# Tokenwise softmax sums: how many of the exponentials GpSimd adds per group, and where the weight bounds are folded

## The reference, cut to what matters

```python
q, k, v = jnp.split(x, 3, axis=1)                      # (64, 32, 512) each
weight = jnp.einsum('bct,bcs->bts', q * scale, k * scale)
weight = jax.nn.softmax(weight, axis=-1)
h = jnp.einsum('bts,bcs->bct', weight, v)              # (64, 32, 512)
h = h + attn(_layernorm(h), Wq, Wk, Wv, Wo, qn_w, kn_w)   # 16 heads, 4 kv heads
h = h + ffn(_layernorm(h), w1, w2, w3)                 # w -> clip(round(w / gamma), -1, 1)
```

## Time and profile before

| | us |
|---|---|
| median of 3 runs | 1106.71 (1106.57 to 1110.37) |
| the profiled execution, its own time | 1115.52 |
| its span, first to last instruction | 1113.7 |
| TensorE busy | 1022.4 (92%) |
| VectorE busy | 713.8 (64%) |
| GpSimd busy | 539.8 (48%) |
| ScalarE busy | 440.5 (40%) |
| granted TensorE clock, mean | 0.956 |

### The profile page before, as it was taken

How to read it: one execution, slowest core, us unless ns; L and a number is a source line. 1 busy time by engine, 2 the same in 40 slices (tenths; PEclk the granted TensorE clock), 3 DMA queues, 4 the chain that set the end, 5 groups by cost and what they waited for, 6 DMA issues and landing times.

```text
span 1113.7 us, 20347 instructions
## 1 busy us (share of the span) xinstructions
PE 1022.4 (92%) x7783; PEld 562.2 (50%) x7783; DVE 713.8 (64%) x1267; ACT 440.5 (40%) x761; POOL 539.8 (48%) x432
## 2 busy tenths in 40 slices
PE   4989889898877599999999999999999999999996
PEld 2433333333322237657466475574765746647554
DVE  6767666778785756557656575575655765657542
ACT  1777675567663423314133232231321313314121
POOL 2576665366688744515435245253451543524500
PEclk9999898889988689999999999999999999999998
DMA  8978785665523001010101001011001010100000
GB/s 236 270 258 253 240 247 164 187 197 179 173 82 100 19 19 30 19 38 19 38 28 28 28 19 38 28 28 38 28 19 38 19 38 28 29 28 19 29 11 20
DMA packets 70436, 92.05 MB, mean 83 GB/s; under 512 B 39296, under 2 KB 39936, under 8 KB 70400
## 3 DMA queue, kind: packets, MB, share of 16 engines
q1 hardware_dynamic: 70400, 91.60, 28.1%
HBM read 49.36 MB, written 8.39 MB: 52 GB/s over the span
## 4 chain that ended last, share of the span: by engine, by line
PE 71%; DVE 9%; issue 7%; POOL 5%; DMA 4%; ACT 2%; SPq 1%; POOLq 0%; DVEq 0%; ACTq 0%
PE ffn_sum L1236 7%; PE ffn_sum L1237 7%; PE proj L1302 5%; PE proj L1303 5%; PE proj L1304 5%; PE tok_out L652 4%; PE score_rows L627 4%; PE proj L1190 3%; PE proj L1192 3%; PE proj L1191 3%; PE score_cols L642 3%; DVE row_max L475 3%; PE transposed L1184 3%; DVE ctx_lo L1090 2%; DMA q_parts<-max_lo 2%
## 5 line engine op out<-in xcount | busy, mean ns | idle before, releaser
L936 POOL TENSOR_TENSOR roped<-rope_cos,rope_sin 128x512 f32<-128x512 f32 x80 | 102.3, 1278 | 230.5 <-DVE rope_sin L1059 230.5
L475 DVE TENSOR_REDUCE row_max<-score_rows 128x1 f32<-128x512 f32 x256 | 163.4, 678 | 57.5 <-PE score_rows L627 57.3
L435 ACT ACTIVATE exps<-score_cols 128x512 f32<-128x512 f32 x256 | 139.6, 601 | 88.0 <-PE score_cols L642 87.0
L1236 PE MATMUL ffn_sum<-x_hi,ffn_w 128*128 128x128 f16 x1408 | 167.1, 220 | 7.7 <-DMA x_lo<-x_lo_rows 7.7
L1237 PE MATMUL ffn_sum<-x_lo,ffn_w 128*128 128x128 f16 x1408 | 166.9, 220 | 0.0
L627 PE MATMUL score_rows<-k_parts,q_parts 96*128 96x512 f32 x256 | 123.5, 497 | 26.2 <-DMA k_parts<-qk_split 14.2
L1236 PEld LDWEIGHTS ffn_sum<-x_hi,ffn_w 128*128 128x128 f16 x1408 | 138.2, 98 | 12.9 <-DMA x_lo<-x_lo_rows 8.2
L1237 PEld LDWEIGHTS ffn_sum<-x_lo,ffn_w 128*128 128x128 f16 x1408 | 138.6, 98 | 2.3
L642 PE MATMUL score_cols<-q_parts,k_parts 98*128 98x512 f32 x256 | 111.2, 443 | 16.5 <-DMA q_parts<-max_lo 11.5
L627 PEld LDWEIGHTS score_rows<-k_parts,q_parts 96*128 96x128 f32 x256 | 53.2, 209 | 119.7 <-DVE row_max L475 62.7
L379 POOL TENSOR_TENSOR exp_sums<-exps 128x512 f32<-128x512 f32 x64 | 82.1, 1313 | 58.7 <-PE score_rows L627 36.2
(11 more groups left out here) (135 smaller groups left out, 1978.8 us busy)
## 6 DMA issues: line engine op xcount, KB each, us to landing
q_parts<-qk_split SPq DMA_DIRECT2D x45, 256.0 KB, 4.2
k_parts<-qk_split SPq DMA_DIRECT2D x45, 256.0 KB, 4.7
attn_slots<-in_w_attn SPq DMA_DIRECT2D x20, 512.0 KB, 6.9
ffn_w<-in_w_ffn SPq DMA_DIRECT2D x13, 704.0 KB, 8.2
qk_split<-in_qk SPq DMA_DIRECT2D x15, 512.0 KB, 6.0
raw_ffn<-in_w_ffn SPq DMA_DIRECT2D x8, 704.0 KB, 5.3
v_t<-in_v_t SPq DMA_DIRECT2D x16, 256.0 KB, 5.6
h_rows<-tok_out_sum SPq DMA_DIRECT2D x16, 256.0 KB, 4.5
```

Of the source, the lines that this page charges most:

```text
L435: nc.scalar.activation(E[:, n % NE, :], ST[n % 3][:, :], ACT.Exp, scale=TOK_SCALE).then_inc(exp_done, 1)
L475: nc.vector.reduce_max(row_max[:, g % 2, k:k + 1], S[n % NS][:, :], AX.X).then_inc(s_free, 1)
L1236: nc.tensor.matmul(dst, w, x2h[:, k, :], start=(k == 0), stop=False)
```

## The change

`DEPTH` is 1 for every group; it was 2 in groups 0 to 7 and in groups 14 and 15. In these ten groups the four `sum_third` of GpSimd go, and `total` has eight matmuls on exponentials in place of four. In the same ten groups the release of round 2 of the exponentials goes from GpSimd's sum to the group's `total`. `fold_bounds` is issued behind the sixth row maximum of its group, it was behind the tenth.

```diff
-        DEPTH = [2] * 8 + [1] * 6 + [2] * 2
+        DEPTH = [1] * NG
@@
-                    if (r, k) == (MEASURES_AT["fold"][0] + 1, MEASURES_AT["fold"][1] + LOOK - 3):
+                    if (r, k) == (MEASURES_AT["fold"][0] + 1, MEASURES_AT["fold"][1] + LOOK - 7):
                         fold_bounds()
```

## The result

The changed kernel took 1096.17 us in the median of 7 runs (1095.93 to 1103.11), the kernel before 1110.37 in 7 (1106.57 to 1111.79). The ratio is 0.9899, 95% interval 0.987 to 0.9928: faster by 1.0%. The profiled execution took 1102.72 us, its span is 1100.9, its mean granted clock 0.972, where the one before had 1115.52, 1113.7 and 0.956. The forecast was 1098.5, between 1092 and 1106.

A forecast was written before the change was run, and what follows sets the result against it. GpSimd was the chain at the tokenwise stage's end; early groups alternated between DMA and TensorE with VectorE. +3.6 - 0.3 - 10.5 = -7.2 on 1106.7 gave 1099.5; one spared clock drop, about 1, made 1098.5, range 1092 to 1106.

The forecast's parts named there:

- Group 14, 4.3 us: End of tokenwise stage: without group 14's thirds GpSimd's chunk 12 starts 4.3 us sooner, not 7.0, as ScalarE is late next.
- Group 15, 6.3 us: GpSimd between chunks 12 and 13: no wait inside, so all 6.3 us of group 15's thirds goes.
- its lower case: End of tokenwise stage: GpSimd's stretching stays, only 5.1 of 6.3 us is saved, and the end gives -9.4.
- The margin behind it: Before the first squares: projections done near 342.5, squares wanted at 342.9; under a microsecond to spare.
- The case that the end gives only 4.3: Rival C: transpose, projections or last sums replace GpSimd as the latest; 1105.7 us, chance 0.22.
- The early additions, +3.6: TensorE sums, groups 0 to 7: 0.88 us each; four paid in full, one 0.08, three hidden by transfers.
- rival B: Clock stays up: all three drops behind DMA-bound groups and the one after the fold spared; 1091 us, chance 0.17.
- the argument on the clock: Group behind a drop took 18.9 us; one at full clock took 17.1 and with its addition would take 18.0.
- The fold, 0.3: VectorE's serial stretch behind the denominators: four reductions move to where VectorE waits for TensorE, saving their length, 0.3 us.
- The clock, -1: TensorE behind DMA-bound groups: shorter waits spare one drop to 1.2 GHz, a gain of about 1 us.
- A: The sum of the parts with one clock drop spared: 1098.5 us, from 1095 to 1102, chance 0.56.

The follow-up runs named there:

- the group by itself: Kernel before with depth 1 in group 14 too, groups 0 to 7 and 15 still at 2: 1105.19 us, ratio 0.9947.
- The early groups alone: Kernel before with depth 1 in groups 0 to 7, fold and groups 14 and 15 as before: 1107.86 us, ratio 0.9975.
- the additions were taken twice: Changed kernel with four more matmuls per group in groups 0 to 7, summing the pairs two times: 1099.47 us, ratio 0.9902.
- the idle products: Changed kernel with six overwritten TensorE products before the first column tile of groups 3, 5 and 7: 1095.41 us, ratio 0.9891.

## Why the prediction was right

**Group 14, 4.3 us: right**, and for the reason given. ScalarE was next (41.8 foretold for the group by itself, 41.8 measured).

**Group 15, 6.3 us: mis-sized.** The thirds went, but 1.4 us came back as a slower chunk 13. The prediction had this as its lower case (-9.4 in all, with the rule on the shared interfaces) and chose -10.5, on the ground that VectorE's instructions would start sooner as well. They did and met the next GpSimd instruction instead. Measured: -9.4.

**The margin behind it: too small.** I had the first projections done half a microsecond before they were wanted. In the changed kernel TensorE went from its last sums straight to them at 335.85, and their twelve products were over by 338.6, 3.2 us before the squares. The case that the end gives only 4.3 fell with it.

**The early additions, +3.6: right in size.** Eight additions cost 4.0 us at equal clock, and seven of them 3.2 in the traces. One reading in the prediction was wrong all the same. It took 17.1 us as the length of a stretch at full clock, to which 0.88 had to be added. That stretch held 0.96 us of waiting, so the base was 16.2 and the length with the addition 17.1, not 18.0. The sum does not hang on it, rival B and the argument on the clock do.

**The fold, 0.3: right.** The wait of 1.47 us went and VectorE was next.

**The clock, -1: mis-sized, and this is the main error.** I counted on one drop being spared. The early groups alone, whose end is as before, had a mean clock of 0.971 against 0.9635, which is worth about 6 us. With it they came out at 0 to 6 us faster and not 3.6 slower. The mechanism was thus between A and B: more was spared than one drop, and less than the 8.5 us of B. The changed kernel's mean clock rose further, from 0.963 to 0.977. About half of that rise is the end (46.1 us at 0.78 became 36.7 at 0.95), and it gives no time beyond the 9.4 us. Why the clock is higher in the early groups alone is not shown. It rose again, to 0.9805, when the additions were taken twice, as it would if work in the waits keeps it up, but the idle products, which were to test this directly, gave no gain that the runs can show.

**The level: luck.** The forecast counted from a median of 3 runs, 1106.71. Over 7 runs the same kernel's median is 1110.37. The change forecast was -8.2 us; measured it is -14.2 between the medians and -11 by the ratio. The parts worked out above make -9.4 - 0.3 + 4 = some -6, and the clock the remaining 5 or more. So 1098.5 against 1096.17 is closer than the sum deserves: the end was 1.1 us too good and the clock some 4 to 5 too small, and the base too low by 3.7 made up for most of that.

## What to carry to other kernels

Judge a chain on an idle-looking engine by the stretch in which the others wait for it: GpSimd was busy for under half of the span, and 8 of the 40 instructions removed shortened the end by 9.4 us. When a stretch's length is used as a price, subtract the waiting in it first, since added work fills that before it costs. And if single executions of one kernel differ by more than the effect, measure a distance between two instructions of one trace; here 46.1 came in three traces and 36.7 to 37.0 in six, while the totals moved by 10. With enough runs the recorded clock helps as well: compared at equal clock, an addition that looked free had a price of 4 us, which the clock returned.

## What the runs showed of the hardware

- A GpSimd subtraction of 128x1024 took 2.13 us alone and 3.51 beside VectorE's ternary instructions; four additions of 128x512 took 5.0 and 7.0. Taken from beside them, both returned to the lower figure.
- TensorE's clock fell behind a wait of 2.73 us in one execution, and behind one of 2.83 at the same place the next tile still ran at 2.4 GHz in another, and the clock fell only after it.
- The kernel before spread over 16 us (1100.6 to 1116.7) with a mean granted clock from 0.974 down to 0.956. Over 57 of its runs 0.001 of mean clock went with 0.84 us.
